# Turning the next group's weights on VectorE in 32x32 blocks instead of on TensorE, and moving the small decay steps

## Chip, cores and metric

One core of a Trainium2 chip runs the whole program. The metric is the device time of one execution in microseconds. The kernel before takes 3421.34 us (median of three runs, 3419.98 to 3421.66).

## What is computed

The input `x` has 128 samples of 32 positions with 512 features, 4096 rows of 512 in all. Three stages follow one another:

1. A small network on `cond_128` gives each sample a 32x32 matrix that mixes its positions; the result is `h`.
2. A state-space layer with `H = 64` heads in `G = 8` groups. Per group it projects `h` by `in_proj_w` to ten chunks of 128 channels (B, C, four of x, four of the gate), runs a causal convolution of four taps and a silu on the first six, scans over the 32 positions with a decay `exp(dt * A)`, gates, normalizes, and multiplies by 512 columns of `out_proj_w`. The sum over groups is added to `x`.
3. A grouped convolution and a feed-forward layer whose weights are looked up by 4-bit or 8-bit codes.

```python
proj = einsum('bld,pd->blp', hidden_states, in_proj_w)
xBC = silu(conv(hbc));  dt_p = softplus(dt + dt_bias);  dA = exp(dt_p * A)
state = state * dA_t + dtx_t * B_t;  y_t = einsum('bhpn,bhn->bhp', state, C_t)
yn = rms_normalized_by_group(y + x * D) * norm_weight * silu(gate)
out = einsum('bli,di->bld', yn, out_proj_w)
```

## The kernel before

Stage 2 is nine tenths of the time. Its loop runs over the eight groups and inside them over eight blocks of 512 rows: 64 equal blocks. Each engine has its own instruction list, and semaphores alone set the order between them. Products keep float32 accuracy by splitting both operands in a high and a low half, three passes each (`PASSES`).

TensorE's order in a block (`tensor_part`, `attend`, L1111) is: six projections n = 0 to 5, the C times B product (L1156), the sums of the decay exponents (L1164, `mask_gtr` with `segr`), three more projections n = 6 to 8, the turning of x (`turn_x`, L1126, 16 transposes), **the turning of the next group's weights** (L1181, eight 128x128 transposes of `stage[0]` and `stage[1]` into two PSUM banks), the scan products (`scan`, L1136), projection n = 9, the output product (L1211, with the sums of squares L1203 between its third and fourth part). In the last group (g = 7) nothing is prepared: L1181 falls away, and the projection n = 8 stands behind `turn_x` (it has `prepare` false).

VectorE's order (`attend`, L1293): four small steps on 128x32 elements that make the decay exponents `adt` and their halves `adts` (L1320, L1323, L1326, L1328), six convolutions of three dependent steps each (L1343), between them the first "leaf" steps of the 8-bit weight lookup (`pair`, L1303, and `find_here`), the masking of C times B before the sixth convolution (L1333), the four scan matrices `m` (L1361), the four `dtx` products from `turn_x`'s banks (L1368), the low halves of the two turned chunks (L1381), then y, z and the low halves of gy (L1393, L1397, L1386), sums of squares, the rest of the lookup (L1311, L1303), and the sum into `acc` (L1438).

ScalarE adds bias and the last tap of each convolution from PSUM (L1252), runs silu (L1234), the decay's exponential (L1258), the gate's silu (L1238), the high halves of the two turned chunks (L1269) and of gy (L1242). GpSimd spreads `adts` over 32 positions, two products of 128x1024 per block (`scan_products`, L1065), and takes the reciprocal root (`root`, L1071).

SyncE issues the transfers in the order of `step` (L989): when the previous block's `acc` is stored, `load_raw` (L983) fetches two chunks of raw weights for the next group into `stage`, each 128 rows of 512 as one transfer; then `acc` is loaded; when L1381 is done both chunks are stored to `wt_d`; then `ht`; at the end `acc` is stored (L1045). `next_chunks` gives chunk 2 + j and, for blocks j = 0 to 3, chunk j % 2, for blocks 4 to 7 one of the four chunks of `out_proj_w`. In block 7 of a group the ten turned chunks of the next group are fetched from `wt_d`.

Stage 1 turns the first group's weights on TensorE (`turn`, L385) and mixes with `xb` as the stationary operand (`mix_chunk`, L440).

Of the kernel before, what the change touches and what calls it, by code (L numbers as in the profile page):

```python
# [25 lines left out]
ds = bass.ds  # L26
# [25 lines left out]
R = 4  # L52
# [72 lines left out]

def weight_rows(a, n, g):
# [8 lines left out]
def mix_part(nc, a, sh, ctx):  # L135
# [89 lines left out]
    s_neg = sem("s1_neg")  # L225
    s_bits = sem("s1_bits")
# [147 lines left out]
    def tensor_part(pe):  # L374

        def turn(n):
# [7 lines left out]
            for k in range(KC):  # L384
                ins = pe.transpose(sh.bank[TURN[n]][:, k * P:(k + 1) * P], raw_chunk(n)[:, k * P:(k + 1) * P], sh.ident[:, :])  # L385
# [95 lines left out]
        for k in range(KC):  # L481
            ins = pe.transpose(p_wdt[:, k * H:(k + 1) * H], wdt[:, k * P:(k + 1) * P], sh.ident[0:H, 0:H])
# [373 lines left out]
def attend_part(nc, a, sh, ctx):  # L856
# [40 lines left out]
    XT, SEG, CB, YB, OUT, SSQ, NEXT = (3, 4, 5, 7), (5, 7), 6, (6, 7, 4, 5), (2, 3, 4, 5), 6, (0, 1)  # L897
# [3 lines left out]
    s_raw = [sem(f"s2_raw{u}") for u in range(2)]  # L901
    s_nps = sem("s2_nps")
# [70 lines left out]
    def sync_part(sp):  # L973
# [84 lines left out]
    def gpsimd_part(pool):  # L1058
        def scan_products(it):

            for half in range(2):
# [11 lines left out]
        scan_products(0)  # L1073
# [12 lines left out]
        for s in range(R):  # L1086
            scan_products(1 + s)
# [13 lines left out]
        with pool.Fori(1 + R, NIT - 1) as it:  # L1101
            scan_products(it)
            root(it)
        scan_products(NIT - 1)
# [5 lines left out]
    def tensor_part(pe):  # L1110
        def attend(g, j, prepare):  # L1111
# [56 lines left out]
            for c in range(CT - 1 if prepare else CT - 2):  # L1168
# [14 lines left out]
            if not prepare:  # L1183
                pe.wait_ge(s_conv, NCV * it + NCV)
                project(NCV + CT - 2)
# [5 lines left out]
            if prepare:  # L1191
                pe.wait_ge(s_nlo, 2 * it + 1)
# [3 lines left out]
            if prepare:  # L1196
                pe.wait_ge(s_nlo, 2 * it + 2)
# [30 lines left out]
    def scalar_part(act):  # L1228
        def attend(g, j, prepare, first=False):
# [17 lines left out]
            for n in range(NCV):  # L1247
# [6 lines left out]
                if 0 < n < NCV - 1:  # L1254
                    silu(n - 1)
            for q in range(SEGB):
# [9 lines left out]
            for u in range(2 if prepare else 0):  # L1266
                act.wait_ge(s_nps, 2 * it + u + 1)
                act.wait_ge(s_nst, 32 * it + 32)
                act.activation(wnext[:, u, 0, :], bank[NEXT[u]][:, :], ACT.Copy).then_inc(s_nhi, 1)  # L1269
# [20 lines left out]
    def vector_part(dve):  # L1290
        lut8 = sh.lut8[:, :, :].rearrange("p t c -> p (t c)").bitcast(I32)
        la, lb, lc, ld = (x[:, :] for x in leaf)
        def attend(wt_tile, gl, j, prepare, first=False):  # L1293
# [19 lines left out]
            def find_here(done):  # L1313
# [5 lines left out]
            dve.wait_ge(s_segr, 2 * it + 2)  # L1319
            dve.tensor_tensor(adt[:, :, :], sh.dt[:, ds(TT * j, TT), ds(HG * g, HG)],  # L1320
                              sh.neg_a[:, ds(HG * g, HG)].unsqueeze(1).to_broadcast([P, TT, HG]), ALU.mult).then_inc(s_adt, 1)
            dve.wait_ge(s_adt, 4 * it + 1)
            dve.tensor_scalar(adt[:, :, :], adt[:, :, :], DECAY_FLOOR, None, ALU.max).then_inc(s_adt, 1)  # L1323
            dve.wait_ge(s_adt, 4 * it + 2)
            adt_v = adt[:, :, :].rearrange("p t h -> p (t h)")
            dve.tensor_copy(adts[:, 0, :], adt_v).then_inc(s_adt, 1)  # L1326
            dve.wait_ge(s_adt, 4 * it + 3)
            dve.tensor_tensor(adts[:, 1, :], adt_v, adts[:, 0, :].bitcast(F32), ALU.subtract).then_inc(s_adt, 1)  # L1328
# [565 lines left out]
```

## Time and profile before

| | before |
|---|---|
| median of three runs | 3421.34 us |
| the profiled execution | 3419.63 us |
| its span, first to last instruction | 3417.9 us |
| stage 1, to the first projection | about 108 us |
| 56 blocks that prepare a next group, then 8 that don't | about 3035 us |
| stage 3 | about 275 us |

The span leaves 1.7 us of the profiled execution outside it, and the profiled execution is 1.7 us below the median. In the timelines a row is a run of like instructions: start, time from the first start to the last end, engine, line, what is written and read, count, and in brackets how long the engine stood idle before and who released it. Starts of instructions that follow each other overlap the end of the one before by up to 0.1 us.

### The profile page before, as it was taken

The numbers are of one execution on the slowest core, as the hardware profiler recorded it, in microseconds if no ns is written. First come the engines' busy times: TensorE is split into PE (matmuls) and PEld (weight loads), VectorE is DVE, ScalarE is ACT, GpSimd is POOL, SyncE is SP. The second block draws the span as 40 slices with busy tenths as digits, with TensorE's granted clock in tenths as the row PEclk, the third lists the DMA queues.
The fourth block names the chain that finished last, engine by engine and source line by source line (L and its number), as shares of the span: only waits on it lengthen the run. The fifth ranks groups of instructions, "written<-read, shape, count | busy, mean of one in ns | idle before, by whom it ended". The sixth has DMA issues, their size and how long they took to land. (4 is left out here: it accounts for less than half of the span.)

```text
span 3417.9 us, 58378 instructions
## 1 busy us (share of the span) xinstructions
PE 3395.8 (99%) x19738; PEld 2869.8 (84%) x19738; DVE 3025.9 (89%) x4815; ACT 1406.9 (41%) x2179; POOL 446.0 (13%) x328
## 2 busy tenths in 40 slices
PE   8999999999999999999999999999999999999999
PEld 6788888888888888888888888888888888888888
DVE  6899999999999999999999999999999999998443
ACT  5555553444434444344443444434444334433111
POOL 1111111011110111101111011110111100111333
PEclk9999999999999999999999999999999999999999
DMA  7433263234432353325433262335423352225331
GB/s 270 172 117 123 105 226 132 107 135 161 159 130 109 135 191 128 131 108 191 136 128 132 107 221 106 127 132 181 148 106 127 131 181 94 76 95 154 93 92 59
DMA packets 207789, 466.23 MB, mean 136 GB/s; under 512 B 35134, under 2 KB 80606, under 8 KB 198284
## 3 DMA queue, kind: packets, MB, share of 16 engines
q1 hardware_dynamic: 206364, 464.72, 38.8%
q0 software_dynamic: 368, 0.85, 0.1%
q10 hardware_dynamic: 1024, 0.27, 0.0%
q8 instruction: 15, 0.25, 0.0%
q14 instruction: 18, 0.15, 0.0%
HBM read 313.68 MB, written 152.09 MB: 136 GB/s over the span
## 5 line engine op out<-in xcount | busy, mean ns | idle before, releaser
L1119 PE MATMUL p_cv<-ht,wt 128*128 128x512 f32 x5376 | 1274.5, 392 | 0.8 <-DVE xc L1343 0.8
L1119 PEld LDWEIGHTS p_cv<-ht,wt 128*128 128x128 f32 x5376 | 1004.0, 188 | 224.3 <-issue 11.0
L1211 PE MATMUL bank<-wot,gy 128*128 128x512 f32 x3072 | 728.3, 392 | 0.0
L1211 PEld LDWEIGHTS bank<-wot,gy 128*128 128x128 f32 x3072 | 571.9, 188 | 121.0
L1252 ACT ACTIVATE xc<-p_cv,cvb,cvw 128x512 f32<-128x512 f32 x256 | 200.0, 782 | 898.6 <-PE p_cv L1119 898.4
L1343 DVE SCALAR_TENSOR_TENSOR xc<-p_cv,cvw,xc 128x496 f32<-128x496 f32 (+2 forms) x768 | 545.0, 717 | 22.1 <-ACT xc L1252 0.2
L1119 PE MATMUL bank<-ht,wt 128*128 128x512 f32 x2304 | 554.6, 390 | 0.0
L1119 PEld LDWEIGHTS bank<-ht,wt 128*128 128x128 f32 x2304 | 431.9, 188 | 89.3
L1071 POOL TENSOR_TENSOR r<-rv,neg_half 128x4 f32<-128x4 f32 x64 | 89.5, 1398 | 2345.0 <-DVE rv L1423 2345.0
L1065 POOL TENSOR_TENSOR segr<-adts,mask_le 128x1024 fp32r<-128x1024 f32 x128 | 243.0, 1920 | 424.0 <-DVE adts L1326 424.0
L1361 DVE TENSOR_TENSOR m<-cbm,y 128x1024 f32<-128x1024 f32 x256 | 295.9, 1218 | 0.0
L1343 DVE SCALAR_TENSOR_TENSOR xc<-bank,cvw,xc 128x496 f32<-128x496 f32 (+2 forms) x384 | 274.5, 715 | 11.2 <-ACT xc L1252 2.2
L1234 ACT ACTIVATE xc<-xc 128x512 f32<-128x512 f32 x384 | 234.5, 627 | 65.2 <-DVE xc L1343 64.0
L1242 ACT ACTIVATE gy<-z 128x512 fp32r<-128x512 f32 x256 | 161.3, 630 | 212.2 <-DVE z L1397 212.2
L1136 PE MATMUL bank<-m,dtx 128*64 128x128 f32 x4096 | 237.7, 274 | 0.0
L1136 PEld LDWEIGHTS bank<-m,dtx 128*64 128x64 f32 x4096 | 222.3, 137 | 12.2 <-issue 12.2
L1368 DVE TENSOR_TENSOR dtx<-bank,dt_all 128x512 f32<-128x512 f32 x256 | 160.4, 684 | 74.3 <-PE bank L1126 74.3
L1397 DVE SCALAR_TENSOR_TENSOR z<-z,nw,y 128x512 f32<-128x512 f32 x256 | 192.4, 752 | 29.8 <-DVE y L1393 5.7
L1393 DVE SCALAR_TENSOR_TENSOR y<-xc,dsk,bank 128x512 f32<-128x512 f32 x256 | 189.6, 741 | 10.4 <-PE bank L1136 10.4
L1685 PE MATMUL p_y<-wq,x3t 128*128 128x512 f32 x768 | 182.9, 394 | 0.0
L1386 DVE TENSOR_TENSOR gy<-z,gy 128x512 fp32r<-128x512 f32 x256 | 175.2, 684 | 0.0
L1438 DVE SCALAR_TENSOR_TENSOR acc<-bank,r,acc 128x512 f32<-128x512 f32 x256 | 173.6, 740 | 0.0
(191 smaller groups left out, 3418.1 us busy)
## 6 DMA issues: line engine op xcount, KB each, us to landing
ht<-h_d SPq DMA_DIRECT2D x63, 2048.0 KB, 7.9
acc_d<-acc SPq DMA_DIRECT2D x64, 1024.0 KB, 4.3
wt_d<-wnext SPq DMA_DIRECT2D x112, 512.0 KB, 3.4
acc<-acc_d SPq DMA_DIRECT2D x56, 1024.0 KB, 7.1
wt<-wt_d SPq DMA_DIRECT2D x70, 512.0 KB, 8.4
stage<-in_L_attn_in_proj_w SPq DMA_DIRECT2D x84, 256.0 KB, 2.8
wot<-wt_d SPq DMA_DIRECT2D x28, 512.0 KB, 6.4
xb<-in_x SPq DMA_DIRECT2D x8, 1024.0 KB, 8.3
```

Source lines behind the costliest of these rows:

```text
L1065: pool.tensor_tensor(segr[:, half, :, :], adts[:, half, :].bitcast(F32).unsqueeze(2).to_broadcast([P, TT * HG, L]), sh.mask_le[:, :].unsqu ...
L1119: ins = pe.matmul(pb[:, :], wt[:, n, l, k, :], ht[:, rr, k, :], start=(q == 0 and k == 0), stop=(q == 2 and k == KC - 1))
L1136: ins = pe.matmul(bank[YB[c]][u * HP:(u + 1) * HP, t * P:(t + 1) * P], dtx[:, t, h * HP:(h + 1) * HP], m[:, h, t, :], start=True, stop=True)
L1211: ins = pe.matmul(bank[OUT[t]][:, :], gy[:, c, l, t * P:(t + 1) * P], wot[:, rr, c, :], start=(c == 0 and q == 0), stop=(c == CT - 1 and q ...
L1234: act.activation(xc[:, n, :], xc[:, n, :], ACT.Silu).then_inc(s_silu, 1)
L1252: act.activation(xc[:, n, :], bank[PROJ_BANK[n]][:, :], ACT.Identity, bias=cvb[:, n:n + 1], scale=cvw[:, n, TAPS - 1:TAPS]).then_inc(s_tap, 1)
L1343: ins = dve.scalar_tensor_tensor(dst, src, cvw[:, n, TAPS - 1 - k:TAPS - k], dst, ALU.mult, ALU.add)
L1361: dve.tensor_tensor(m[:, :, t, :].rearrange("p h (c l) -> p h c l", l=L), cbm[:, t, :].rearrange("p (c l) -> p c l", l=L).unsqueeze(1).to_ ...
L1386: dve.tensor_tensor(gy[:, c, 1, :], z[:, c, :], gy[:, c, 0, :].bitcast(F32), ALU.subtract).then_inc(s_ulo, 1)
L1393: dve.scalar_tensor_tensor(y[:, c, :], xc[:, 2 + c, :], dsk[:, c:c + 1], bank[YB[c]][:, :], ALU.mult, ALU.add).then_inc(s_y, 1)
L1397: dve.scalar_tensor_tensor(z[:, c, :], z[:, c, :], nw[:, c:c + 1], y[:, c, :], ALU.mult, ALU.mult).then_inc(s_u, 1)
L1685: ins = pe.matmul(p_y[t % 2][q][:, :], x3t[:, l, t, r, :], wq[:, q, rr, r, :], start=(n == 0 and r == 0), stop=(n == 2 and r == R - 1))
```

## The change

The inner dimension of all weights is dealt out to the four pieces of 128 by remainder instead of by block: piece k holds columns 4c + k (`inner_columns`). In stage 1 the stationary operands of the turning, of the mixing and of the small `wdt` turning are therefore read with a step of four elements.

In stage 2 the next group's weights are no longer turned on TensorE. The loads are split so that the 32-row pieces land in exchanged partition groups: four transfers per input chunk (pieces of 512 bytes), and sixteen transfers per chunk of `out_proj_w` (pieces of 128 bytes), of which SyncE waits for the first twelve before it issues the last four. VectorE then transposes 32x32 blocks of both chunks from SBUF to SBUF between `m` and `dtx`, ScalarE takes the high halves and VectorE the low halves from there. For input chunks the transpose reads with a step of four elements, for output chunks in runs of 32. TensorE takes the order of the last group everywhere: n = 8 behind `turn_x`.

Of the four small decay steps only the floor stays on VectorE. GpSimd makes `adt` (behind `root` of the block before) and the low half; ScalarE makes the high half behind the second tap and the first silu. So the two large products of GpSimd start after ScalarE's copy. VectorE's loop over eight blocks becomes two loops over four, and GpSimd's one loop becomes loops over groups and blocks.

```diff
+def inner_columns(src, k):
+    return src.rearrange("p (q c) -> p c q", c=KC)[:, k, :]
...
-                ins = pe.matmul(p_h[k][:, t * P:(t + 1) * P], xb[j % 2][:, t, k * P:(k + 1) * P], mix[:, TT * block_at(j) + t, :],
+                ins = pe.matmul(p_h[k][:, t * P:(t + 1) * P], inner_columns(xb[j % 2][:, t, :], k), mix[:, TT * block_at(j) + t, :],
...
         def load_raw(g, j):
             for u, n in enumerate(next_chunks(j)):
-                sp.dma_start(stage[u][:, :], weight_rows(a, n, g)).then_inc(s_raw[u], 16)
+                src = weight_rows(a, n, g)
+                for m in range(P // L):
+                    if n < NPJ:
+                        sp.dma_start(stage[u][m * L:(m + 1) * L, :].rearrange("p (m x) -> p m x", x=P),
+                                     src[:, m * P:(m + 1) * P].rearrange("(m p) x -> p m x", p=L)).then_inc(s_raw[u], 16)
+                        continue
+                    parts = src[m * L:(m + 1) * L, :].rearrange("p (c b e) -> b p c e", c=KC, e=L)
+                    if m == P // L - 1:
+                        sp.wait_ge(s_rawout, 16 * (P // L - 1) * (P // L) * (KC * (g - 1) + j - (NBLK - KC) + 1))
+                    for b in range(P // L):
+                        sp.dma_start(stage[u][b * L:(b + 1) * L, m * P:(m + 1) * P].rearrange("p (c e) -> p c e", e=L),
+                                     parts[b]).then_inc(s_rawout if m < P // L - 1 else s_raw[u], 16)
...
+            pool.wait_ge(s_segr, 2 * it + 2)
+            pool.tensor_tensor(adt[:, :, :], sh.dt[:, ds(TT * j, TT), ds(HG * g, HG)],
+                               sh.neg_a[:, ds(HG * g, HG)].unsqueeze(1).to_broadcast([P, TT, HG]), ALU.mult).then_inc(s_adt, 1)
+            pool.wait_ge(s_adt, 4 * it + 3)
+            pool.tensor_tensor(adts[:, 1, :], adt_v, adts[:, 0, :].bitcast(F32), ALU.subtract).then_inc(s_adt, 1)
...
-            for c in range(CT - 1 if prepare else CT - 2):
+            for c in range(CT - 2):
...
-            for u in range(2 if prepare else 0):
-                pe.wait_ge(s_raw[u], 16 * it + 16)
-                pe.wait_ge(s_z, CT * it + CT + 1 + u)
-                for k in range(KC):
-                    ins = pe.transpose(bank[NEXT[u]][:, k * P:(k + 1) * P], stage[u][:, k * P:(k + 1) * P], sh.ident[:, :])
-                ins.then_inc(s_nps, 1)
...
+            project(NCV + CT - 2)
...
+                if n == 1:
+                    act.wait_ge(s_adt, 4 * it + 2)
+                    act.activation(adts[:, 0, :], adt[:, :, :].rearrange("p t h -> p (t h)"), ACT.Copy).then_inc(s_adt, 1)
...
-                act.activation(wnext[:, u, 0, :], bank[NEXT[u]][:, :], ACT.Copy).then_inc(s_nhi, 1)
+                act.activation(wnext[:, u, 0, :], wnext[:, u, 1, :].bitcast(F32), ACT.Copy).then_inc(s_nhi, 1)
...
+            for u in range(2 if prepare else 0):
+                dve.wait_ge(s_raw[u], 16 * (P // L) * it + 16 * (P // L))
+                dve.transpose(wnext[:, u, 1, :].bitcast(F32).rearrange("p (k m e) -> p m k e", k=KC, e=L),
+                              stage[u][:, :].rearrange("p (m k e) -> p m k e" if u == 1 and out_rows else "p (m e k) -> p m k e",
+                                                       k=KC, e=L)).then_inc(s_nps, 1)
             for t in range(TT):
                 times_dt(t)
...
-                dve.tensor_tensor(wnext[:, u, 1, :], bank[NEXT[u]][:, :], wnext[:, u, 0, :].bitcast(F32),
+                dve.tensor_tensor(wnext[:, u, 1, :], wnext[:, u, 1, :].bitcast(F32), wnext[:, u, 0, :].bitcast(F32),
                                   ALU.subtract).then_inc(s_nlo, 1)
```

## Rows read from the trace of the kernel before

**Rows 1.** The page's part 1: busy time, share of the span, instructions.

```profile
PE 3395.8 (99%) x19738; PEld 2869.8 (84%) x19738; DVE 3025.9 (89%) x4815; ACT 1406.9 (41%) x2179; POOL 446.0 (13%) x328
```

**Rows 2.** The store of acc that ends each block: 47 preparing blocks, 7 last ones.

```profile
L1045 SPq DMA_DIRECT2D acc_d<-acc x47: 387/393/2174, 540.8 to 2724.3; - x47
L1045 SPq DMA_DIRECT2D acc_d<-acc x7: 378/378/388, 2817.9 to 3097.4; - x7
```

**Rows 3.** Timeline of one preparing block, from its n = 0.

```profile
1485.79 5.65 PE L1119 MATMUL p_cv<-ht,wt 128*128 128x512 f32 x24
...
1512.79 2.53 DVE L1368 TENSOR_TENSOR dtx<-bank,dt_all 128x512 f32<-128x512 f32 x4 [1.33 <-PE bank L1126]
...
1513.90 1.04 PE L1181 MATMUL p_cv<-ident,stage 128*128 128x128 f32 x8
...
1514.86 3.71 PE L1136 MATMUL bank<-m,dtx 128*64 128x128 f32 x64
...
1516.45 0.74 DVE L1393 SCALAR_TENSOR_TENSOR y<-xc,dsk,bank 128x512 f32<-128x512 f32 x1
...
1518.51 3.03 PE L1119 MATMUL p_cv<-ht,wt 128*128 128x512 f32 x12
```

**Rows 4.** Timeline of one block of the last group, from its n = 0.

```profile
3000.32 4.06 PE L1119 MATMUL p_cv<-ht,wt 128*128 128x512 f32 x17
...
3009.54 2.22 DVE L1343 SCALAR_TENSOR_TENSOR xc<-bank,cvw,xc 128x496 f32<-128x496 f32 x3 [0.32 <-ACT xc L1252]
...
3025.91 2.47 DVE L1368 TENSOR_TENSOR dtx<-bank,dt_all 128x512 f32<-128x512 f32 x4
...
3028.54 3.71 PE L1136 MATMUL bank<-m,dtx 128*64 128x128 f32 x64
```

**Rows 5.** STREAM_TRANSPOSE in stage 1, and two engines reading its output with a step.

```profile
18.15 1.31 DVE L730 STREAM_TRANSPOSE turned<-p_cv 128x512 f32<-128x512 f32 x2 [1.87 <-PE p_cv L420]
...
L261 DVE COPY mix<-turned x4: 371/376/390, 19.5 to 36.1; 32x256 f32<-32x256 f32 x4
...
L270 ACT ACTIVATE mix<-turned 32x256 f32<-32x256 f32 x4 | 2.6, 653 | 4.9 <-DVE turned L730 4.9
```

**Rows 6.** The block of rows 3 in its convolution part, and two later leaf steps.

```profile
1489.98 0.17 DVE L1320 TENSOR_TENSOR adt<-dt_all,neg_a 128x32 f32 x1
...
1490.74 4.36 DVE L1343 SCALAR_TENSOR_TENSOR xc<-p_cv,cvw,xc 128x496 f32<-128x496 f32 x6
1490.75 3.80 POOL L1065 TENSOR_TENSOR segr<-adts,mask_le 128x1024 fp32r<-128x1024 f32 x2 [5.14 <-DVE adts L1326]
...
1493.00 0.63 ACT L1234 ACTIVATE xc<-xc 128x512 f32<-128x512 f32 x1 [0.74 <-DVE xc L1343]
...
1497.15 0.54 DVE L1303 TENSOR_SCALAR stage<-mask,lut 128x512 int32<-128x512 int32 x1
...
1497.73 2.22 DVE L1343 SCALAR_TENSOR_TENSOR xc<-p_cv,cvw,xc 128x496 f32<-128x496 f32 x3
...
1502.60 0.54 DVE L1303 TENSOR_SCALAR leaf<-mask,lut 128x512 int32<-128x512 int32 x1
...
1503.25 0.69 DVE L1333 TENSOR_TENSOR cbm<-bank,mask_cb 128x512 f32<-128x512 f32 x1
...
1530.43 0.99 DVE L1303 TENSOR_SCALAR leaf<-mask,lut 128x512 int32<-128x512 int32 x2
```

**Rows 7.** Groups by shape (busy us, mean ns | idle before): GpSimd's small products.

```profile
L1095 POOL TENSOR_TENSOR cbq<-cbn,gmask 32x32 f32<-32x32 f32 x36 | 8.3, 261 | 0.3
```

**Rows 8.** SyncE: start of a block's load_raw; eight 32-partition loads; their time to landing.

```profile
1494.61 0.35 SPq L985 DMA_DIRECT2D stage<-in_L_attn_in_proj_w  x1
...
3114.98 4.19 SPq L1016 DMA_DIRECT2D x2p<-acc_d  x8
...
x2p<-acc_d SPq DMA_DIRECT2D x64, 128.0 KB, 3.3
```

**Rows 9.** Eight turnings at the start of stage 3, read with a step of four elements.

```profile
3146.07 1.20 PE L1662 MATMUL p_y<-ident,w_nat 128*128 128x128 f32 x8 [0.48 <-PEq L1480]
```

More of the change, by code:

```diff
@@ L225, in mix_part @@
     s_neg = sem("s1_neg")
+    sh.s_dt, sh.s_neg = s_dt, s_neg
     s_bits = sem("s1_bits")
@@ L384, in turn @@
             for k in range(KC):
-                ins = pe.transpose(sh.bank[TURN[n]][:, k * P:(k + 1) * P], raw_chunk(n)[:, k * P:(k + 1) * P], sh.ident[:, :])
+                columns = inner_columns(raw_chunk(n), k) if n < NPJ_ALL else raw_chunk(n)[:, k * P:(k + 1) * P]
+                ins = pe.transpose(sh.bank[TURN[n]][:, k * P:(k + 1) * P], columns, sh.ident[:, :])
             ins.then_inc(s_wps, 1)
@@ L481, in tensor_part @@
         for k in range(KC):
-            ins = pe.transpose(p_wdt[:, k * H:(k + 1) * H], wdt[:, k * P:(k + 1) * P], sh.ident[0:H, 0:H])
+            ins = pe.transpose(p_wdt[:, k * H:(k + 1) * H], inner_columns(wdt[:, :], k), sh.ident[0:H, 0:H])
         ins.then_inc(s_pe, 1)
@@ L1071, in root @@
             pool.tensor_tensor(r[:, :], rv[:, :], sh.neg_half[:, 0:TT], ALU.pow).then_inc(s_r, 1)
-        scan_products(0)
+        pool.wait_ge(sh.s_dt, NBLK // 2)
+        pool.wait_ge(sh.s_neg, 4)
+        scan_products(0, 0)
         pool.wait_ge(s_segr, 4)
@@ L1086, in gpsimd_part @@
         for s in range(R):
-            scan_products(1 + s)
+            scan_products(0, 1 + s)
             pool.wait_ge(s_segr, 2 * s + 6)
@@ L1100, in gpsimd_part @@
             root(1 + s)
[L1101 to L1104, printed above, removed]
+        with pool.Fori(1 + R, NBLK) as j:
+            scan_products(0, j)
+            root(j)
+        with pool.Fori(1, G - 1) as g:
+            with pool.Fori(0, NBLK) as j:
+                scan_products(g, j)
+                root(NBLK * g + j)
+        with pool.Fori(0, NBLK - 1) as j:
+            scan_products(G - 1, j)
+            root(NBLK * (G - 1) + j)
+        scan_products(G - 1, NBLK - 1)
         pool.wait_ge(s_proj, NPJ * (NIT - 1) + 7)
@@ L1292, in vector_part, with attend @@
         la, lb, lc, ld = (x[:, :] for x in leaf)
-        def attend(wt_tile, gl, j, prepare, first=False):
+        def attend(wt_tile, gl, j, prepare, first=False, out_rows=False):
             g = G // OT * wt_tile + gl
@@ L1439, in attend @@
                                          ALU.mult, ALU.add).then_inc(s_acc, 1)
-        with dve.Fori(0, NBLK) as j:
-            attend(0, 0, j, True, first=True)
-        with dve.Fori(0, NBLK) as j:
-            attend(0, 1, j, True)
+        HALVES = ((0, NBLK - KC, False), (NBLK - KC, NBLK, True))
+        for lo, hi, out_rows in HALVES:
+            with dve.Fori(lo, hi) as j:
+                attend(0, 0, j, True, first=True, out_rows=out_rows)
+        for lo, hi, out_rows in HALVES:
+            with dve.Fori(lo, hi) as j:
+                attend(0, 1, j, True, out_rows=out_rows)
         for wt_tile in range(1, OT):
             with dve.Fori(0, G // OT - (wt_tile == OT - 1)) as gl:
-                with dve.Fori(0, NBLK) as j:
-                    attend(wt_tile, gl, j, True)
+                for lo, hi, out_rows in HALVES:
+                    with dve.Fori(lo, hi) as j:
+                        attend(wt_tile, gl, j, True, out_rows=out_rows)
         with dve.Fori(0, NBLK) as j:
```

25 lines of the change are left out of this document (7 added, 18 removed).

## The prediction

> **What bounds the kernel now.** I read the page's busy times first [rows 1]: TensorE is busy in 99% of the span, VectorE in 89%. So only work taken from TensorE can shorten the loop, and VectorE has little room to take it up. The stores of acc then give the length of a block [rows 2]: (2724.3 - 540.8) / 46 = 47.47 us where a next group is prepared, (3097.4 - 2817.9) / 6 = 46.58 us in the last group. The second figure is the one to find: the last group already runs TensorE's new order, with no turning of weights and n = 8 behind turn_x. The ceiling of the change is therefore 0.88 x 56 = 50 us, if nothing takes TensorE's place.
>
> Then the timeline of a block of either kind, counted from the start of its n = 0. Preparing block [rows 3]: dtx at 27.00, after 1.33 idle; turning of the weights at 28.11, scan at 29.07, y at 30.66, n = 9 at 32.72. Last group [rows 4]: dtx at 25.59 with no idle, scan at 28.22. VectorE's third convolution stands there 0.32 us idle for ScalarE's tap and starts at 9.22. Stop at that row: a VectorE that is early can't use it, since from the third convolution on it is tied to the taps, and they come when TensorE's projections do.
>
> **The change, part by part.** *TensorE* loses eight turnings, 0.96 us from 28.11 to 29.07 [rows 3]; the last group shows the same gain as 0.88 per block [rows 2].
>
> *VectorE* gets two transposes of 128x512. The one such pair in the trace took 1.31 us for both, from PSUM and without a step [rows 5]. Three of four of the new ones (both in blocks 0 to 3, one in blocks 4 to 7) read SBUF with a step of 16 bytes, which no row has. The nearest reads the tile `turned` with a step of 128 bytes: VectorE's copy of 256 elements took 0.376 us, ScalarE's 0.653 [rows 5]. So I bound a stepped transpose by 0.60 and, were it slowed as ScalarE is against VectorE, 0.65 x 0.653 / 0.376 = 1.13 us. I take 0.65, from the row of the same engine; the other end is a rival. Less than a transpose without a step it can't cost.
>
> The Trainium skill, "SBUF — State Buffer", section "Door 1: The DMA port swizzle", says that SBUF is read in lines of 16 bytes and that an access which crosses to a new line pays a penalty. By it stepped transposes are dear; ScalarE's row agrees with it and VectorE's doesn't.
>
> The transposes stand between m and dtx, where 1.33 us were idle, and seem hidden. But that idle time was VectorE waiting for turn_x, and turn_x now comes earlier: in the last group dtx has no idle before it and ends at 25.59 + 2.47 = 28.06 [rows 4]. With the pair ahead of it, it ends at 29.37. The first part of the scan takes the four dtx tiles in turn and wants the last at 28.22 + 12/64 x 3.65 = 28.90. So TensorE waits 0.47, with 0.05 for the semaphore 0.52, and a block takes 46.58 + 0.52 = 47.10: of 0.88 us 0.37 are kept. The other 0.79 us of the transposes lie under turn_x and n = 8. ScalarE's high halves follow the gate of n = 8, the low halves as before, and y starts at about 30.7, as it did.
>
> *The small steps.* Four took 1490.74 - 1489.98 = 0.76 us [rows 6]; with the floor alone some 0.12 are left, 0.64 go. By the tie to the taps they are worth nothing in themselves; they take up lateness at the start of a block. ScalarE's copy of 32 columns, 0.2 us at most by VectorE's 0.17 for the same size [rows 6], fits between silu and the next tap. GpSimd's two steps have four times the partitions and the same 32 columns as its product of 0.26 us [rows 7]; I take that, between 0.2 and 0.5. The first of them stands behind root. All of VectorE's convolutions are queued behind the wait for it, but it has 4 us to come.
>
> *What GpSimd's large products now meet.* Before, they ran 1490.75 to 1494.55, beside convolution steps only; the first leaf step came at 1497.15, or 11.36 in the block [rows 6]. Now they follow ScalarE's copy. From y to the next convolution VectorE needs 1490.74 + 47.47 - 1516.45 = 21.76, less 0.64 = 21.12. In a block of 47.2 us the convolution so starts at 30.7 + 21.12 - 47.2 = 4.6; silu 2.26 later [rows 6], ended at 7.5; copy to 7.65; semaphore and low half to 8.05; products 3.80, to 11.85. They overlap the leaf step by 0.5 us. No row shows the two together, so a leaf step waits between nothing and 0.5 (0.9 if GpSimd's small steps are slow). I take the full 0.5: the step moves 512 elements and leaves after 0.99 - 0.54 = 0.45 us [rows 6], a dtx tile after 0.62 [rows 4], so it does more than one element at a time and likely uses a path that GpSimd needs.
>
> Most of it is absorbed. The step leaves after 0.45, but its convolution starts 1497.73 - 1497.15 = 0.58 later, at the tap: 0.13 of slack. The next leaf step repeats that, and before cbm it is 1503.25 - 1502.60 - 0.45 = 0.20 [rows 6]. Together 0.46. What stays is 0.04; but a shorter block starts its convolution later against TensorE, and the sums meet at a block of about 47.20. So 0.27 us per block, 15 us, are kept.
>
> The Trainium skill, "SBUF — State Buffer", section "Who interferes with whom", says that VectorE's modes with two ports and GpSimd share a pair of ports and that the first to start holds it for its whole instruction. By that rule the sum is the one with the wait, without it the one of rival A. No row of before shows it.
>
> *SyncE.* load_raw starts at 1494.61 - 1485.79 = 8.82 in a block [rows 8]. Eight 32-partition loads took 4.19 us to issue, 0.55 each, and 3.3 us to land [rows 8]. Blocks 0 to 3: eight issues, landed by 17, free. Blocks 4 to 7: sixteen issues, the last landed at 17.2 + 3.3 = 20.5; the wait; four more, landed at 25.3 to 25.7. VectorE wants that chunk at 25.6 + 0.65 = 26.25. It fits by about 0.7 us, and I cost it at nothing. Queued behind SyncE's wait are the load of acc (issued by 23, used at 49) and, in block 7, the reloads of wt; they and ht should land before the next block. Behind VectorE's wait for the chunk stand dtx and so the scan.
>
> *Stage 1.* 256 mixing records and 44 turnings load their stationary operand with a step. Eight stepped turnings took 1.20 us [rows 9], eight plain ones 1.04 [rows 3]: 0.023 each, 7 us of TensorE. Stage 1 is not TensorE's alone; I take 3, between 0 and 10.
>
> Sum for the profiled execution: 3419.63 - 15 + 3 = 3407.6. The median lay 1.7 above it: 3409.
>
> **The rivals.** *A: the leaf step isn't held.* 56 x 0.37 = 21 us go, with stage 1: 3403. For it: GpSimd slows nothing in the trace. Against: the leaf step's rate.
>
> *B: stepped transposes are dear.* Each 0.48 more, 1.5 of them per block on average: 0.72 us, all on the way from m to the scan. The block takes 47.92 against 47.47 before: 25 us more, with stage 1 28 more, 3449. It decides from 0.27 / 1.5 = 0.18 us per stepped transpose; this is how the kernel gets slower. For it: ScalarE's row. Against: VectorE's.
>
> *C: the output chunk is late.* Were an issue 0.65 instead of 0.55, or a landing 1 us longer, twice in a row, VectorE would wait 0.8 to 1.3 us in 28 blocks: 22 to 36 us, 3438.
>
> *D: the whole ceiling comes.* Were the scan's start free of dtx, 50 us would go, 3374. Against: dtx's own arithmetic.
>
> **How the numbers follow.** The forecast 0.44, its own range 3398 to 3420 (GpSimd's small steps 0.2 to 0.5, a transpose 0.60 to 0.70, stage 1 0 to 10); A 0.17; B 0.19; C 0.17; D 0.03. Changes within 0.2% (7 us) can't be told from none. The forecast puts 0.34 on faster, 0.09 on same, 0.01 on slower; A 0.16 and 0.01; B, with costs in between, 0.02, 0.03 and 0.14; C 0.02, 0.04 and 0.11; D faster. Together faster 0.57, same 0.17, slower 0.26. The range takes in A, and B and C but for their upper ends: 3395 to 3448.
>
> **What would show it.** In the profile of after: the transposes at 1.3 us the pair; dtx ending at 29.4 in a block, and the scan waiting 0.5 in its first quarter; the third convolution still at 9.2; the leaf step at 11.36 ending 0.5 late; blocks of 47.2 us by the stores. Wrong would be a scan without a wait (D), a leaf step of 0.54 with the products still running beside it (A), stepped transposes of 1.1 us (B), VectorE waiting for a load ahead of the second transpose in blocks 4 to 7 (C).

## The result, and the profile after

The changed kernel takes 3449.47 us (median of three runs, 3449.35 to 3452.42) against 3421.34: ratio 1.0086, 95% interval 1.0066 to 1.0106. It is slower by about 28 us, on the side that the prediction held less likely and 1.5 us outside its range. The profiled execution took 3449.47 us with a span of 3447.7, so 29.8 us are to be found between the two spans.

First the page's part 1 of the kernel after (engine, busy us, share, instructions), then its DMA line:

```profile
PE 3412.4 (99%) x19290; PEld 2842.6 (82%) x19290; DVE 3087.6 (90%) x4735; ACT 1404.8 (41%) x2243; POOL 474.0 (14%) x456
...
DMA packets 304596, 466.59 MB, mean 135 GB/s; under 512 B 103230, under 2 KB 191710, under 8 KB 295052
```

Against [rows 1] TensorE has 448 instructions less and is busy 16.6 us longer. An engine that does less and takes longer for it is a sign to look at the length of its instructions, not at waits alone. (Not all of the rise is length: the page's scan products are busy for 270.1 us instead of 237.7, at a mean of 278 ns instead of 274, so they mostly stand further apart.) The DMA packets rise from 207789 to 304596, since the loads come in smaller pieces; experiment 4 keeps these pieces. TensorE's timeline where stage 1 ends:

```profile
106.07 4.00 PE L447 MATMUL p_cv<-mix,xb 128*128 128x128 f32 x16
...
130.42 5.73 PE L1154 MATMUL p_cv<-ht,wt 128*128 128x512 f32 x24
```

The same two places in the kernel before:

```profile
99.08 2.05 PE L440 MATMUL p_cv<-mix,xb 128*128 128x128 f32 x16
...
108.16 5.73 PE L1119 MATMUL p_cv<-ht,wt 128*128 128x512 f32 x24
```

Sixteen mixing products take 4.00 us instead of 2.05, and the first projection comes 22.3 us later. That is three quarters of the loss. The weight loads of the mixing (ns: least, median, most) say why; first after, then before:

```profile
L447 PEld LDWEIGHTS p_cv<-mix,xb x128: 308/330/330, 24.5 to 123.3; 128*128 128x128 f32 x128
```

```profile
L440 PEld LDWEIGHTS p_cv<-mix,xb x128: 186/192/333, 24.3 to 100.7; 128*128 128x128 f32 x128
```

The load of the stationary operand, read with a step of 16 bytes, takes 330 ns in the median instead of 192.

The rest of the loss is in stage 2. SyncE's stores of acc, the first pair with two input chunks in the block, the second pair with one:

```profile
1422.28 0.39 SPq L1064 DMA_DIRECT2D acc_d<-acc  x1
1470.01 0.39 SPq L1064 DMA_DIRECT2D acc_d<-acc  x1
...
1564.82 0.39 SPq L1064 DMA_DIRECT2D acc_d<-acc  x1
1612.21 0.39 SPq L1064 DMA_DIRECT2D acc_d<-acc  x1
```

Blocks 0 to 3 take 47.7 to 47.8 us, blocks 4 to 7 47.4, against 47.47 [rows 2]. From the first store of acc to the last it is 3173.83 - 184.65 = 2989.18 us against 3143.98 - 161.15 = 2982.83: 6.3 more. The very first block, from the first projection to its store, is 1.2 longer, which I did not follow further. In sum, 22.3 + 1.2 + 6.3 = 29.8.

One block with two stepped transposes, in its scan part (start, length, engine, line, idle before and releaser). Its n = 0 starts at 1417.79:

```profile
1427.01 2.22 DVE L1360 SCALAR_TENSOR_TENSOR xc<-bank,cvw,xc 128x496 f32<-128x496 f32 x3 [0.41 <-ACT xc L1275]
...
1438.84 4.62 DVE L1378 TENSOR_TENSOR m<-cbm,y 128x1024 f32<-128x1024 f32 x4
...
1443.38 2.04 DVE L1397 STREAM_TRANSPOSE wnext<-stage 128x512 f32<-128x512 f32 x2
1445.35 2.44 DVE L1385 TENSOR_TENSOR dtx<-bank,dt_all 128x512 f32<-128x512 f32 x4
1446.14 0.95 PE L1171 MATMUL bank<-m,dtx 128*64 128x128 f32 x8
...
1447.24 0.44 PE L1171 MATMUL bank<-m,dtx 128*64 128x128 f32 x4 [0.16 <-DVE dtx L1385]
...
1447.84 3.06 PE L1171 MATMUL bank<-m,dtx 128*64 128x128 f32 x52 [0.16 <-DVE dtx L1385]
...
1450.83 1.42 PE L1154 MATMUL p_cv<-ht,wt 128*128 128x512 f32 x5
```

The pair takes 2.04 us, not 1.31 as the pair of [rows 5]. dtx ends at 30.0 in the block, not at 28.06 as in [rows 4]; the scan starts on the first tiles and then waits for each next one; n = 9 comes at 33.0, where the kernel before had it at 32.72 [rows 3]. The whole list of transposes (ns: least, median, most), and the pair of a block where one is stepped and one reads in runs:

```profile
L1397 DVE STREAM_TRANSPOSE wnext<-stage x112: 666/1061/1080, 157.9 to 2776.5; 128x512 f32<-128x512 f32 x112
```

```profile
1633.35 1.67 DVE L1397 STREAM_TRANSPOSE wnext<-stage 128x512 f32<-128x512 f32 x2
```

### The profile page after: what moved, and what is told of

The parts are those of the page before. It is cut to its first block and busy times, and to the rows that moved or that the text cites. A ratio compares the mean times of both kernels' runs of the same rounds, so it can differ in the third digit from the quotient of the medians.

```text
span 3447.7 us, 59396 instructions
## 1 busy us (share of the span) xinstructions
PE 3412.4 (99%) x19290; PEld 2842.6 (82%) x19290; DVE 3087.6 (90%) x4735; ACT 1404.8 (41%) x2243; POOL 474.0 (14%) x456
## 2 busy tenths in 40 slices
DMA packets 304596, 466.59 MB, mean 135 GB/s; under 512 B 103230, under 2 KB 191710, under 8 KB 295052
## 5 line engine op out<-in xcount | busy, mean ns | idle before, releaser
L1171 PE MATMUL bank<-m,dtx 128*64 128x128 f32 x4096 | 270.1, 278 | 22.2 <-DVE dtx L1385 18.6
L1328 DVE TENSOR_SCALAR leaf<-mask,lut 128x512 int32<-128x512 int32 x320 | 167.0, 539 | 0.0
```

Source lines behind the costliest of these rows:

```text
L1171: ins = pe.matmul(bank[YB[c]][u * HP:(u + 1) * HP, t * P:(t + 1) * P], dtx[:, t, h * HP:(h + 1) * HP], m[:, h, t, :], start=True, stop=True)
```

## The experiments

The comparison in each ran beside the kernel before, whose median was 3419.99 to 3421.15 in the four sets.

**1. Stage 1 of the change alone.** The kernel before with the stepped operands of stage 1.

```diff
-  ins = pe.matmul(p_h[k][...], xb[j % 2][:, t, k * P:(k + 1) * P], mix[...])
+  ins = pe.matmul(p_h[k][...], inner_columns(xb[j % 2][:, t, :], k), mix[...])
```

> The kernel before with only stage 1 of the change: the stationary operands of the turnings, of the mixing and of the wdt turning are read with a step of four elements; stage 2 is as before, so h and the weights no longer agree and the output is not the reference's. In the trace of the changed kernel the first projection starts at 130.4 us instead of 108.2. Theory (stepped loads of the stationary operand cost it all): the first projection at about 131, blocks of 47.47 us, and 3421.3 + 22.3 = 3444 us. Rival (stage 1 is late for another reason, such as the changed transfers or the moved first decay step): the first projection at 109 to 112, 3422 to 3426 us.

Measured: 3443.37 us, ratio 1.0069 (1.0052 to 1.0086); first projection at 130.15; blocks unchanged at 47.47. The 22 us of stage 1 are there by themselves.

**2. The turnings of stage 1 alone.** Only the 40 turnings of input chunks are stepped, the mixing is not.

> The kernel before with only the 40 turnings of stage 1 read with a step (mixing and wdt plain; output not the reference's). Theory (a turning loads its operand in one pass and a step adds 0.02 us to it, the mixing loads it twice per product and pays 0.12 us per record, 31 us in all): 3421 to 3422 us. Rival (the turnings pay as the mixing does, 0.12 each and more on the path): 3424 to 3428 us.

Measured: 3420.59 us, ratio 0.9999 (0.999 to 1.0009), first projection at 108.17. The turnings cost nothing. The four small turnings of `wdt` are plain here, but in experiment 5 they are stepped by four while the mixing is not, and the first projection starts at 108.51: the mixing is all of it.

**3. The change with a plain stage 1.** The change with `inner_columns` taken back in stage 1.

> The changed kernel with stage 1 read without a step again; stage 2 as changed (output not the reference's, for the two orders of the inner dimension no longer agree). Theory: stage 1 gives back 22 us, blocks stay at 47.77 (two stepped transposes) and 47.42 (one): 3449.5 - 22.3 = 3427 us. Rival (stage 1 is late for another reason): 3445 us or more.

Measured: 3428.22 us, ratio 1.0022 (1.0012 to 1.0031), first projection at 108.81, blocks 47.77 and 47.40. So stage 2 of the change is by itself 7 us slower than before.

**4. And the transposes in runs of 32.**

```diff
-  stage[u][:, :].rearrange("p (m k e) -> p m k e" if u == 1 and out_rows else "p (m e k) -> p m k e", ...)
+  stage[u][:, :].rearrange("p (m k e) -> p m k e", ...)
```

> As e2, and the block transposes read runs of 32 elements in all blocks (the output is not the reference's). Theory: a transpose of 128x512 takes 0.67 us instead of 1.06, dtx ends 0.8 or 0.4 us earlier, and blocks take 47.1 us, as the prediction reckoned for plain transposes: 3427 - 56 x 0.5 = 3399 us, 0.994 of before. Rival (the scan is late because of the products, the small pieces or the loop in halves): transposes get shorter, blocks stay above 47.4, 3415 to 3427 us.

Measured: 3403.70 us, ratio 0.9952 (0.9935 to 0.9968), blocks of 47.15. Its transposes:

```profile
L1397 DVE STREAM_TRANSPOSE wnext<-stage x112: 665/686/709, 136.1 to 2730.3; 128x512 f32<-128x512 f32 x112
```

With transposes of 0.69 us the block is what the prediction's arithmetic gave for a pair of 1.31 without a held leaf step, 47.10, within 0.05. The model of the block stands; two prices put into the sum were wrong. The rival fell: neither the small pieces nor the loop in halves nor the moved products keep the blocks above 47.4.

**5. How wide a step may be.** The change with its step of four elements (16 bytes) made two (8 bytes), in the mixing and in every transpose.

```diff
-  inner_columns(xb[j % 2][:, t, :], k)
+  xb[j % 2][:, t, (k // 2) * 2 * P:(k // 2 + 1) * 2 * P].rearrange("p (q c) -> p c q", c=2)[:, k % 2, :]
```

> The kernel after with every step of four elements (16 bytes) in the mixing's stationary operand and in the two transposes replaced by a step of two (8 bytes), all 112 transposes; it leaves out the right order of columns. Line theory: what costs is the number of 16-byte lines that an operand touches, 1/4 line per element in runs, 1/2 at a step of two, 1 at a step of four. Then a transpose takes 0.67 + (1.06 - 0.67)/3 = 0.80 us, a weight load of the mixing 192 + (329 - 192)/3 = 238 ns, stage 1 loses about 7 us instead of 22, blocks take about 47.10 + 0.26 = 47.4: 3449.5 - 15 - 13 = 3421. Step theory: any step costs the same, whatever its width: transposes 1.06 us in all 56 blocks, blocks of 47.77, stage 1 as in the kernel after: 3449.5 + 28 x 0.37 = 3460. A step theory the other way (only a full line per element costs): transposes 0.67, loads 192 ns, 3404 to 3410.

Measured: 3403.90 us, ratio 0.9952 (0.9935 to 0.9969): that of experiment 4, where nothing is stepped. Transposes and weight loads:

```profile
L1397 DVE STREAM_TRANSPOSE wnext<-stage x112: 665/686/706, 136.0 to 2729.9; 128x512 f32<-128x512 f32 x112
...
L447 PEld LDWEIGHTS p_cv<-mix,xb x128: 193/196/331, 24.2 to 101.2; 128*128 128x128 f32 x128
```

Neither the count of 16-byte lines nor the step as such has a price in proportion: a step of 8 bytes costs nothing on the transpose and 4 ns on the load (196 against 192), one of 16 bytes adds 0.38 us to 0.69 and 138 ns to 192. The third of the expectations held. The Trainium skill, "SBUF — State Buffer", section "Door 1: The DMA port swizzle", says that two accesses to each 16-byte line are needed for full rate. These runs agree: at 8 bytes there are two float32 elements of an operand in a line, at 16 bytes one. The same passage says that each access which crosses to a new line pays a penalty, and the prediction leaned on that; at 8 bytes twice as many accesses cross as in runs, and the runs show no price for it.

**6. The small steps back on VectorE,** all else as in the change.

> The changed kernel with the three small decay steps back on VectorE. Theory (VectorE waits for ScalarE's tap ahead of its third convolution by 0.4 us in a block, and three later small waits of 0.13 to 0.2 follow): 0.64 us more at the start of a block are absorbed, 3449 us, within 4 us of the changed kernel. Rival one (VectorE is the bound, and every step taken from it counts): 0.64 x 64 = 41 us slower, 3490. Rival two (the moved steps hold VectorE up, since the large products now run later): up to 20 us faster, 3430.

Measured: 3457.32 us, ratio 1.0107 (1.0091 to 1.0124), 8 us more than the kernel after and outside the 4 us that the theory allowed; but the blocks are the same 47.77 and 47.40. By the stores the difference is one block of 53.5 us. The waits name it:

```profile
DVE adt L1337 <- issue: 6.2, 1, 6.2
```

VectorE stood 6.2 us at the first of the four steps at the start of one block, with nothing in the profile that released it; TensorE waited 5.3 us of it. Stage 1 took 0.75 more. They are no price of the steps, which would be paid in 64 blocks. What they are is open. The trace has two 8 KB packets of its instruction queue at 2043.0 and 2043.4, inside the wait (2040.7 to 2046.9), and six between 2041 and 2056, where the starts of other groups have two or three; that suggests a wait for instructions, but no run tests it. In a block the steps are worth nothing on either side.

**7. GpSimd's products right onto the leaf step.** ScalarE's copy a tap later, so that the products start 2.4 us later and cover the whole leaf step.

```diff
-  if n == 1:
+  if n == 2:
       act.activation(adts[:, 0, :], adt[...], ACT.Copy).then_inc(s_adt, 1)
```

> The changed kernel with ScalarE's copy of the decay behind the third tap and second silu instead of the second and first, so that GpSimd's two large products run from about 10.3 to 14.1 us in a block and VectorE's first leaf step at 11.36 falls into the first of them. In the changed kernel they overlap by 0.14 us only. Theory of the prediction (the leaf step can't run beside GpSimd): it starts 0.8 us late or more, of which 0.46 are absorbed; blocks 0.35 us longer or more, 3469 us and above, or GpSimd's products get longer instead. Rival (they don't disturb each other): leaf step 0.54 us at 11.36, products 1.92 each, 3449 us.

Measured: 3451.39 us, ratio 1.0089 (1.0072 to 1.0106), blocks as after. VectorE's and GpSimd's rows there:

```profile
1617.88 3.98 POOL L1091 TENSOR_TENSOR segr<-adts,mask_le 128x1024 fp32r<-128x1024 f32 x2
...
1619.12 0.95 DVE L1328 TENSOR_SCALAR stage<-mask,lut 128x512 int32<-128x512 int32 x1
1620.00 2.21 DVE L1360 SCALAR_TENSOR_TENSOR xc<-p_cv,cvw,xc 128x496 f32<-128x496 f32 x3
```

And the same in the kernel after:

```profile
1615.47 3.79 POOL L1091 TENSOR_TENSOR segr<-adts,mask_le 128x1024 fp32r<-128x1024 f32 x2
...
1619.12 0.54 DVE L1328 TENSOR_SCALAR stage<-mask,lut 128x512 int32<-128x512 int32 x1
1619.71 2.22 DVE L1360 SCALAR_TENSOR_TENSOR xc<-p_cv,cvw,xc 128x496 f32<-128x496 f32 x3
```

The total says "no hold", the rows say otherwise. The leaf step is held for 0.41 us in all but the first block, where it is 0.69: it starts while the first product has 0.68 to go and ends 0.28 after it. The two products together take 0.19 longer. Neither total of the expectation came. The convolution behind it starts 0.29 late, and at cbm nothing is left of it: cbm starts at 1625.22 in both kernels. So the hold exists, and the slack at the taps takes it up, as the prediction reckoned (0.46). In the kernel after the products end at 11.50 in the block and the leaf step starts at 11.36: nothing is held, but for the first block.

**8. Both kinds of chunk in pieces of 128 bytes, loads ahead of their block, stage 1 plain.** A version without a stepped read.

```diff
+  parts = weight_rows(a, next_chunks(j)[u], g).rearrange("(m p) (c b e) -> m b p c e", p=L, c=KC, e=L)
+  for m in range(P // L):
+      for b in range(P // L):
+          sp.dma_start(stage[u][b * L:(b + 1) * L, m * P:(m + 1) * P]..., parts[m, b])
...
-  load_raw(nxt, j)            # at the start of the block
+  load_next(nxt, j, 0)        # behind ht
+  load_next(nxt, j, 1)        # behind the store of acc
```

> The reference's output again. Stage 1 as in the kernel before (inner dimension in pieces of 128 columns); both chunks are loaded in pieces of 128 bytes, sixteen transfers each with no wait between them, and issued one block earlier: the first chunk behind the load of ht, the second behind the store of acc. VectorE transposes runs of 32 in the place that the change gave it; the decay steps are moved as in the change. Theory (the stepped reads were the only costs that the change need not have): blocks of 47.15 us as in e3, 3404 us, 0.995 of before. Rival (32 issues and 4096 pieces of 128 bytes per block crowd the queue, so that ht or acc comes late): 3415 to 3450 us, and TensorE waits for ht or VectorE for acc.

Measured: 3422.15 us, ratio 1.0005 (0.9995 to 1.0015), 18 us above experiment 4. Its blocks are 47.16 as there, but the last block of a group with the first of the next takes 54.7 + 41.8 = 96.5 us by the stores instead of 94.3. In that stretch:

```profile
1645.34 1.13 PE L1191 MATMUL bank<-xc 128*128 128x128 f32 x8 [0.87 <-DMA wot<-wt_d]
...
1658.07 0.95 PE L1171 MATMUL bank<-m,dtx 128*64 128x128 f32 x8 [0.73 <-DVE dtx L1385]
```

TensorE waits twice, 1.6 us. Together the seven ends of groups are 16.0 us longer than in experiment 4, which is most of the 18: 5.0 at the first, 1.5 to 2.2 at the others. SyncE's list there, and TensorE's waits for wot over the whole run (us, times, longest):

```profile
1616.69 12.00 SPq L994 DMA_DIRECT2D stage<-in_L_attn_in_proj_w  x16
...
1631.79 8.19 SPq L1055 DMA_DIRECT2D wot<-wt_d  x4
```

```profile
PE bank L1191 <- DMA wot<-wt_d: 7.5, 7, 3.1
```

SyncE is busy for 12 us with issuing one chunk's sixteen transfers, and the reload of wot goes out behind them, at 51.0 in the block, where experiment 4 has it at 47.4. The rival of the expectation held, though it named ht and acc and it is wot that is late, and the second chunk of the next block.

**9. The transposes behind dtx,** the low halves behind the first y and z; loads as in experiment 8.

```diff
+  for t in range(TT):
+      times_dt(t)
   for u in range(2 if prepare else 0):
       dve.transpose(...)
-  for t in range(TT):
-      times_dt(t)
```

> As e9, and on VectorE the two transposes stand behind the four dtx products instead of ahead of them, and the two low halves behind the first y and z. Theory (what held the blocks at 47.15 instead of the last group's 46.58 is that the scan waits for dtx behind the transposes, and VectorE is idle 1.30 us ahead of y in the last group): the scan starts without a wait and blocks take 46.6 to 46.8 us: 3404 - 56 x 0.45 = 3379 us, 0.988 of before. Rival (VectorE as a whole has become the bound, wherever the transposes stand): blocks stay at 47.1, 3400 to 3404 us.

Measured: 3408.36 us, ratio 0.9963 (0.995 to 0.9975). The scan no longer waits; yet the blocks are 47.0 to 47.2, not 46.6: the theory fell, and the rival's length of a block held. TensorE in such a block:

```profile
1321.71 3.71 PE L1171 MATMUL bank<-m,dtx 128*64 128x128 f32 x64
...
1330.70 2.60 PE L1234 MATMUL bank<-wot,gy 128*128 128x512 f32 x10 [0.27 <-DVE y L1413]
```

The wait has moved to the output product, which needs the halves of gy that VectorE now makes later. The waits of that kernel show it over the whole run (us, times, longest):

```profile
PEld bank L1234 <- DVE y L1413: 36.5, 56, 0.8
PE bank L1234 <- DVE y L1413: 9.1, 33, 0.4
```

Against experiment 8 the stretch from the first store of acc to the last is 10.8 us shorter, and 7.5 of these lie in the seven ends of groups. VectorE's transposes waited 6.5 us for their loads in experiment 8, and here they don't. Moving a piece of VectorE's chain within the chain gains next to nothing.

**10. The low halves on GpSimd,** one edit to experiment 9.

```diff
+  def low_halves(it):          # GpSimd, ahead of root
+      for u in range(2):
+          pool.wait_ge(s_nhi, 2 * it + u + 1)
+          pool.tensor_tensor(wnext[:, u, 1, :], wnext[:, u, 1, :].bitcast(F32), wnext[:, u, 0, :].bitcast(F32), ALU.subtract)
```

> The kernel with the transposes behind dtx and loads ahead (3408.4 us, blocks of 47.04 us), with one edit: the low halves of both turned chunks move from VectorE to GpSimd, behind its large products and ahead of the reciprocal root. Theory V: what bounds that kernel is no longer the start of the scan but VectorE's chain from the x banks to the low halves of gy (dtx 2.48, transposes 1.29, y and z, the two low halves 1.29, the halves of gy), for which TensorE's output product waits 0.27 and its weight loads 0.7. With 1.29 us less on VectorE the block falls to the last group's 46.58, so 56 x 0.47 = 26 us go: 3382. Theory P (GpSimd's tensor work holds VectorE): two products of 128x512, 1.30 us each by stage 3's product of that shape, hold VectorE for as long as they run: VectorE gains nothing, or loses up to 1.3, blocks of 47.1 to 48.3, 3408 to 3470. Theory S (the scan's start was the bound and still is): 3408, no change.

Measured: 3384.27 us, ratio 0.9891 (0.9875 to 0.9908). The stores stand 46.58 apart, the last group's block [rows 2]:

```profile
1288.79 0.41 SPq L1058 DMA_DIRECT2D acc_d<-acc  x1
1335.37 0.40 SPq L1058 DMA_DIRECT2D acc_d<-acc  x1
1381.95 0.40 SPq L1058 DMA_DIRECT2D acc_d<-acc  x1
```

Theory V held: the chain from the x banks to gy was the bound, and 1.29 us less of it frees TensorE wholly in such a block.

**11. The low halves on GpSimd, but the transposes still ahead of dtx:** the same edit to experiment 4.

> The kernel with stage 1 plain and both transposes in runs of 32, ahead of dtx (3403.7 us, blocks of 47.15 us), with one edit: the low halves of both turned chunks on GpSimd. It leaves out the agreement of the order of columns between stages. The prediction's arithmetic: the block is lengthened by dtx standing behind the transposes, 0.52 us at the start of the scan, which this edit does not touch. TensorE has lost that time before the low halves come: blocks stay at 47.10 to 47.15, 3404. Rival: VectorE's total work is the bound, then 1.3 us less of it gives blocks of 46.6 and 3376. If GpSimd holds VectorE, blocks get longer, 47.2 to 48.4.

Measured: 3410.78 us, ratio 0.9972 (0.996 to 0.9983): 7 us *more* than experiment 4, though VectorE has less to do. Blocks of 47.04 to 47.46. The rows of one:

```profile
1318.28 3.06 PE L1181 MATMUL bank<-m,dtx 128*64 128x128 f32 x52 [0.16 <-DVE dtx L1395]
1318.49 2.51 POOL L1097 TENSOR_TENSOR wnext<-wnext 128x512 fp32r<-128x512 f32 x2 [17.82 <-ACT wnext L1304]
1318.87 0.75 DVE L1423 SCALAR_TENSOR_TENSOR y<-xc,dsk,bank 128x512 f32<-128x512 f32 x1 [0.64 <-PE bank L1181]
1319.72 1.83 DVE L1427 SCALAR_TENSOR_TENSOR z<-z,nw,y 128x512 f32<-128x512 f32 x1
```

z takes 1.83 us instead of 0.75: it is held until GpSimd's second product ends at 1321.00, and is done 0.55 later. y, which has one of its two tensors in PSUM, runs beside GpSimd in its usual 0.75. So GpSimd takes 1.08 us from VectorE at the worst place, in front of gy. The third of the expectations held, but not in every block. One of 47.04:

```profile
844.41 3.03 POOL L1097 TENSOR_TENSOR wnext<-wnext 128x512 fp32r<-128x512 f32 x2 [18.33 <-ACT wnext L1304]
844.69 0.75 DVE L1423 SCALAR_TENSOR_TENSOR y<-xc,dsk,bank 128x512 f32<-128x512 f32 x1 [0.54 <-PE bank L1181]
845.55 0.75 DVE L1427 SCALAR_TENSOR_TENSOR z<-z,nw,y 128x512 f32<-128x512 f32 x1
```

Here GpSimd starts 0.28 before y instead of 0.38, z gets in before the second product and takes 0.75, and it is GpSimd's pair that is longer, 3.03. In all blocks of the groups 2 to 5 the first z takes 1.82 or 1.83 and a block 47.4 to 47.5 us; in those of groups 1 and 6 it takes 0.75 and a block 47.0 to 47.1, which is 0.1 less than in experiment 4. A tenth of a microsecond in who comes first decides over 0.42 us per block, and the groups with the held z make the run slower than experiment 4. In experiment 10 GpSimd starts 0.07 after y; z then gets its turn between the two products, and two z of one block are held for 0.28 and 0.19 only, GpSimd's pair for 0.47:

```profile
1267.25 2.98 POOL L1097 TENSOR_TENSOR wnext<-wnext 128x512 fp32r<-128x512 f32 x2 [19.20 <-ACT wnext L1304]
1268.04 1.03 DVE L1427 SCALAR_TENSOR_TENSOR z<-z,nw,y 128x512 f32<-128x512 f32 x1
...
1269.84 0.94 DVE L1427 SCALAR_TENSOR_TENSOR z<-z,nw,y 128x512 f32<-128x512 f32 x1
```

The Trainium skill, "SBUF — State Buffer", section "Who interferes with whom", says that an instruction of VectorE with two inputs in SBUF contends with a GpSimd instruction that reads SBUF, and that one with at most one such input, outside the modes with two ports, does not. z and y agree with the two halves of it here.

**12. A step of two, loads in their own block.** The findings in one version: columns dealt with a step of 8 bytes within windows of 256, input chunks in pieces of 256 bytes, transposes behind dtx, low halves on GpSimd.

```diff
-  return src.rearrange("p (q c) -> p c q", c=KC)[:, k, :]
+  return src.rearrange("p (h q c) -> p h c q", h=2, c=2)[:, k // 2, k % 2, :]
```

> A version with the right output that puts the findings together: columns dealt with a step of two (8 bytes) within windows of 256, so that the input chunks come in 256-byte pieces in eight transfers and no load runs a block ahead; output chunks in sixteen transfers as in the kernel after; transposes behind dtx, low halves on GpSimd. From the kernel with loads ahead and low halves on GpSimd (3384.3 us, its groups' ends about 0.8 us long each): if the crowding of the DMA queues by 128-byte pieces is what lengthens the ends of groups, seven times 0.8 go: 3378, blocks of 46.6, first projection at 108.8. Rival 1: the last block of each group is late for another reason, the cost stays, 3384. Rival 2 (loads): blocks 4 to 7 now issue 8 + 16 loads, 2.2 us more than in the kernel after; if the last lands after 28.1 in the block, VectorE waits and 28 blocks get longer by 0.5 us or more: 3398. Rival 3: a transpose whose input has five dimensions costs more than 0.68 us: 1.06 as at a step of 16 bytes would make VectorE's chain late by 0.4 to 0.8, blocks of 46.8 to 47.0, 3390 to 3400.

Measured: 3388.77 us, ratio 0.9909 (0.9893 to 0.9926), beside experiment 10 the same within the intervals. First projection at 107.94, blocks of 46.58, transposes with that input of 0.69 us. The gain at the ends of groups did not come: against 63 blocks of 46.585 us (2934.9), first to last store of acc take 2950.9 here and 2947.9 in experiment 10. Here the first end costs nothing and the other six are 2.0 to 3.4 us too long; in experiment 10 the first is 5.3 too long and the others 0.7 to 1.9, not 0.8 each as the expectation had it. In this version it is the load of ht that is late, behind SyncE's 24 transfers and the reloads of wt:

```profile
PE p_cv L1165 <- DMA ht<-h_d: 13.4, 6, 2.5
```

ht goes out at 37.1 to 37.6 in the last block of these groups, and at 35.7 in the kernel after, whose block is also 0.8 us longer. So the ends of groups cost about as much with 256-byte pieces in the group's last block as with 128-byte pieces ahead of it, by another transfer. That it is SyncE's time to issue, and not the size of the pieces, is argued from these starts; no run varies one without the other. Experiments 10 and 12 are 1% faster than the kernel before and 1.8 to 1.9% faster than the change.

## Why the prediction was wrong

**Right: the model of the block.** *What bounds the kernel* put TensorE first and named 46.58 as the block to reach; experiment 10 reached it. The third convolution was to stay at the tap at 9.2: it starts at 1427.01 - 1417.79 = 9.22, after 0.41 idle. dtx behind the transposes was to hold up the scan for 0.52, giving 47.10: with transposes of 0.69 (experiment 4) it is 47.15. With the true price of the pair, 2.04 instead of 1.31, the same sum moves n = 9 and the rest by 0.73; measured is 47.77 against 47.10 + 0.73 = 47.83, and for one stepped transpose 47.40 against 47.10 + 0.36 = 47.46.

**Wrong: the term for stage 1.** It said 3 us, between 0 and 10; it is 22.3, and this alone would have put the result outside the forecast's own range. The step that failed: I priced 256 mixing loads from [rows 9], where eight stepped turnings take 1.20 us. By these rows the step costs (1.20 - 1.04) / 8 = 0.020 each (the prediction wrote 0.023), here (4.00 - 2.05) / 16 = 0.122, and 256 of them are 31 us; by the busy times of the mixing, 64.5 us against 36.8, it is 28, of which 22 reach the first projection. A turning of 128 columns takes about 0.13 to 0.15 us, a plain mixing product of the same size 0.13 too; but the row that I used is a total of eight instructions, and it doesn't show the time of the load alone. The trace of the kernel before had that time, for the same stepped turnings and for plain ones:

```profile
L1662 PEld LDWEIGHTS p_y<-ident,w_nat x8: 195/209/218, 3146.0 to 3146.9; 128*128 128x128 f32 x8
...
L1181 PEld LDWEIGHTS p_cv<-ident,stage x448: 140/141/142, 137.3 to 2748.6; 128*128 128x128 f32 x150
```

A stepped load is half as long again there, 68 ns more, and most of it is hidden; that was the warning to see. The mixing's load starts from 192 ns and gains 138, and there it isn't hidden. Experiment 2 shows how little the turnings tell of the mixing: in the same stage their step costs nothing at all in time. Why a turning's load gains less than a mixing load no run here explains.

**Wrong: the price of a stepped transpose.** I took 0.65 us, from VectorE's copy with a step of 128 bytes, and gave the dear end, 1.13 by ScalarE's row, to rival B. Measured: 1.06. Rival B was right in mechanism and place (on the way from m to the scan) and within 0.07 in price; its total, 3449, is the measured one by two errors that cancel. It set 1.5 x 0.48 = 0.72 on a block of 47.20, 47.92; the pair took 2.04 and 1.67, and the mean block is 47.59, so that 56 blocks lose 6.7 us and not 25. Its 3 us in stage 1 were 22. The copy's row was the wrong neighbour: same engine, other instruction. That ScalarE was 1.7 times slower on the same reads should have had more weight than 0.19.

**Partly right: the held leaf step.** The hold exists (0.41 us in experiment 7) and the slack takes it up, both as written. But the products start at 7.71 and end at 11.50, not at 8.05 and 11.85: VectorE's convolution, ScalarE's copy and the hand-over to GpSimd each come a little earlier. In the kernel after nothing is held. In experiment 4, whose block is as short as the prediction's, the products end at 11.70 and the leaf step does take 0.60 to 0.71 us in 54 blocks, not 0.54; with a block of 47.15 against 47.10, at most 0.05 of the 0.10 that I put on each block is there.

**Right: what was costed at nothing.** The small steps are worth nothing in a block (experiment 6). Rival C didn't happen: SyncE's sixteen issues for the output chunk end at 20.1 in the block, their last landing near 22, against the 26.25 at which VectorE would want it:

```profile
1618.79 9.10 SPq L1003 DMA_DIRECT2D stage<-in_L_attn_out_proj_w  x16
```

Rival D, the scan's start free of dtx, fell in two steps: experiment 9 freed the scan and gained almost nothing in a block, since VectorE's chain goes on to gy. That second end of the chain stands nowhere in the prediction.

Put together, 3419.6 + 22.3 (stage 1) + 1.2 (first block) + 6.3 (stage 2) = 3449.4. Against the prediction's 3407.6, stage 1 is 19.3 too low in the sum, and stage 2 with the first block, where it had 15 us kept and 7.5 were lost, 22.5.

## What to carry to other kernels

Before an operand gets a step, count how many of its elements share 16 bytes: with two the reads here were free, with one they cost half as much again on VectorE's transpose and about 70% on TensorE's weight load; so deal columns by two and not by four. Price an unknown by the row of the same instruction, and if there is none, let the dearest engine's row decide the middle of the range. When a wait of the bounding engine is taken away, follow the other engine's chain to the next place where it is waited for: only moving work off VectorE, not along it, gave TensorE its time back, and only with the transposes behind dtx (experiment 11).

## What the runs showed of the hardware

- A float32 read of SBUF with a step of 16 bytes: STREAM_TRANSPOSE of 128x512 1.06 us against 0.69; load of a 128x128 stationary operand of the mixing 330 ns against 192, of a turning 209 against 141 (medians). With a step of 8 bytes: 0.69 us, and 196 ns for the mixing.
- GpSimd holds VectorE, and is held by it: beside a GpSimd product a product of VectorE with both inputs in SBUF went from 0.75 to 1.83 us and ended 0.55 after GpSimd's, the leaf step went from 0.54 to 0.95, a GpSimd pair from 2.51 to 2.98; a product with an input in PSUM was not slowed (0.75). Which of the two is held turned on 0.1 us (experiment 11).
- Many small transfers are not free where a group's weights are reloaded: sixteen took SyncE 12.0 us to issue, and TensorE waited for what stood behind them, for wot (7.5 us in seven waits, experiment 8) or for ht (13.4 in six, experiment 12). The ends of groups were up to 6 us too long.
- VectorE once stood 6.2 us at the start of a block with nothing that released it (experiment 6).
